# A time-warping kernel: lanes side by side instead of interleaved, one wait for the whole table, edge padding written first

## The reference

```
x = x + _L0_xattn_ref(ctx_1024, _layernorm(x))     # alignment by dynamic time warping
x = x + _L0_attn_ref(_layernorm(x), ...)           # a recurrence over time
x = x + _L0_ffn_ref(_layernorm(x), ...)            # 8 experts, 2 for each row, and a shared one
```

```
R[i, j] = D[i, j] + min(R[i-1, j], R[i, j-1], R[i-1, j-1])
```

## Time and profile before

| | us |
|---|---|
| median of three runs | 1157.94 |
| the three runs | 1157.61, 1157.94, 1163.07 |
| the profiled execution | 1163.07, of which its span 1161.8 |
| busy: PE, DVE, ACT, POOL | 1008.3, 660.2, 494.6, 116.0 |
| chain that ended last: PE, DVE, DMA | 58%, 27%, 5% |

### The profile page before, as it was taken

How to read it: one execution, slowest core, us unless ns; L and a number is a source line. 1 busy time by engine, 2 the same in 40 slices (tenths; PEclk the granted TensorE clock), 3 DMA queues, 4 the chain that set the end, 5 groups by cost and what they waited for, 6 DMA issues and landing times.

```text
span 1161.8 us, 15564 instructions
## 1 busy us (share of the span) xinstructions
PE 1008.3 (87%) x4892; PEld 599.0 (52%) x4892; DVE 660.2 (57%) x2312; ACT 494.6 (43%) x847; POOL 116.0 (10%) x150
## 2 busy tenths in 40 slices
PE   5887779888881999967989699887999999999998
PEld 2332233333330555533766465556676767676776
DVE  4987889999999774686679312447211111111116
ACT  4886647767760545323321364332222222222221
POOL 1000000000000000000000000000343434342110
PEclk9999889999995999989889798897999999999999
DMA  9999764655758998250140393783222212123014
GB/s 355 262 315 358 246 213 142 185 162 169 234 180 282 286 300 249 82 163 0 30 159 1 120 357 115 193 323 118 67 71 67 75 61 81 57 85 107 28 59 177
DMA packets 123887, 189.76 MB, mean 163 GB/s; under 512 B 9232, under 2 KB 93360, under 8 KB 123808
## 3 DMA queue, kind: packets, MB, share of 16 engines
q1 hardware_dynamic: 117920, 170.41, 45.4%
q0 software_dynamic: 5888, 18.36, 5.0%
HBM read 165.43 MB, written 23.30 MB: 162 GB/s over the span
## 4 chain that ended last, share of the span: by engine, by line
PE 58%; DVE 27%; DMA 5%; issue 4%; ACT 3%; SPq 2%; POOL 0%; DVEq 0%; ACTq 0%; POOLq 0%
PE bank L1824 13%; PE bank L1671 8%; PE bank L1855 7%; PE bank L1692 5%; DVE table L832 4%; PE bank L1816 3%; PE bank L1835 3%; DVE beyond L848 2%; PE bank L1847 2%; DVE passed L853 2%; PE bank L1598 2%; DVE col_min L825 2%; DMA spaced<-dist 2%; DVE z L762 2%; PE bank L1599 2%
## 5 line engine op out<-in xcount | busy, mean ns | idle before, releaser
L1036 DVE TENSOR_TENSOR hid<-bank,act_s 128x352 f32<-128x352 f32 x104 | 54.2, 523 | 221.1 <-PE bank L1824 182.2
L1824 PE MATMUL bank<-w_up,srcT 128*128 x512 | 162.8, 460 | 0.7 <-ACT srcT L1442 0.7
L1450 ACT ACTIVATE act_s<-bank 128x352 f32<-128x352 f32 x104 | 48.1, 464 | 200.7 <-PE bank L1824 127.6
L1582 PE MATMUL bank<-sq,ones 128*64 128x402 f32 (+1 forms) x512 | 103.6, 527 | 30.1 <-ACT sq L1299 30.1
L1824 PEld LDWEIGHTS bank<-w_up,srcT 128*128 128x128 f32 x512 | 96.0, 189 | 47.9 <-issue 4.1
L1576 PE MATMUL bank<-ctxT,latT 128*64 128x402 f32 (+1 forms) x512 | 103.1, 525 | 6.0 <-DMA ctxT<-ctx_tr_dram 5.2
L1598 PE MATMUL bank<-table,ident 128*128 128x402 f32 x144 | 66.0, 541 | 47.1 <-DVE stays L795 41.6
L1299 ACT ACTIVATE sq<-ctxT 128x1608 f32<-128x1608 f32 x64 | 97.5, 1527 | 9.9 <-DMA ctxT<-ctx_tr_dram 9.9
L1671 PE MATMUL bank<-rows_c,on_path 128*64 128x256 f32 (+1 forms) x832 | 99.0, 389 | 2.2 <-DMA rows_c<-ctx_nat_dram 1.4
L1855 PE MATMUL bank<-w_dn,hidT 128*128 (+1 forms) x384 | 93.6, 380 | 0.4 <-DVE y_sb L1050 0.4
L832 DVE TENSOR_TENSOR_SCAN table<-col_min,table 128x201 f32<-128x201 f32 x140 | 88.6, 633 | 2.7
(11 more groups left out here) (293 smaller groups left out, 1625.0 us busy)
## 6 DMA issues: line engine op xcount, KB each, us to landing
rows_c<-ctx_nat_dram SPq DMA_DIRECT2D x32, 896.0 KB
ctxT<-ctx_tr_dram SPq DMA_DIRECT2D x32, 804.0 KB, 7.1
ctxT<-ctx_tr_dram SPq DMA_DIRECT2D x32, 797.0 KB, 7.0
rows_c<-ctx_nat_dram SPq DMA_DIRECT2D x32, 640.0 KB
spaced<-dist SPq DMA_DIRECT2D x128, 101.0 KB, 3.4
table<-spaced SPq DMA_DIRECT2D x64, 202.0 KB, 4.0
w_up<-w_t_dram SPq DMA_DIRECT2D x16, 704.0 KB, 12.6
w_dn<-w_t_dram SPq DMA_DIRECT2D x16, 256.0 KB, 5.3
```

The source lines that it names most:

```text
L1036: e.tensor_tensor(hid[i][:, :], psum[2 * i + 1][:, 0:HH], act_s[i][:, :], ALU.mult).then_inc(hid_done, 1)
L1582: last = e.matmul(ps[b * T:(b + 1) * T, 0:nq], ones[:, 0:T], sq[i][:, b, k, 0:nq], start=False, stop=(k == KC - 1))
L1824: last = e.matmul(psum[2 * i + m][:, 0:HH], srcT[t % 2][:, k, :], w_up[:, bass.ds(ex, 1), m, k, columns], start=(k == 0), stop=(k == KC - 1))
```

## The change

Three things change together.

1. **Lanes.** A batch's 8 segments now stand in 8 neighbouring partitions: partition p holds segment p % 8 of batch p // 8. The shuffles' tables (`LEFT`, `RIGHT`, `FIRST_LANE`) and the few instructions that derive a lane's segment and batch from its number follow; one DVE instruction on 128 x 1 is gone (`SHAPED` 14 to 13). A table load now writes neighbouring partitions: after pair 3 the 64 partitions 0 to 63 by one DMA for each 8 rows instead of two, after the others 32.
2. **One semaphore for the table.** `table_in` counts all pieces of a group together, and `align` waits once, before its first step, until all of them have landed.
3. **Padding.** `far` has 128 partitions of 7 * 202 numbers instead of 16 of 8 * 202. Two DMAs write the first 7 rows and the last 7 rows of every lane of `spaced`, before any distance, and the first store of a distance waits for them. `load_table` no longer waits for the padding.

```diff
-QUADS = P // 32
-SETS = GB // QUADS
-
-LEFT = [(lane - SETS) % 32 for lane in range(32)]
-RIGHT = [(lane + SETS) % 32 for lane in range(32)]
-FIRST_LANE = [lane % SETS for lane in range(32)]
+LEFT = [lane - 1 if lane % SEGS else lane + SEGS - 1 for lane in range(32)]
+RIGHT = [lane + 1 if lane % SEGS < SEGS - 1 else lane - SEGS + 1 for lane in range(32)]
+FIRST_LANE = [lane // SEGS * SEGS for lane in range(32)]
...
-PAD = SEGS * W
+PAD = (SEGS - 1) * W
...
-        TABLE_IN = [16 * SETS * (g + 1) for g in range(GROUPS)]
-        PADDED = 16 * (SEGS - 1)
+        TABLE_IN = [16 * -(-STEPS // FEW_ROWS) * sum(len(sets) for sets in LOADED_WITH[:g + 1]) for g in range(GROUPS)]
+        PADDED = 16 * 2
...
-            e.memset(far[0:GB, :], BIG).then_inc(filled, 1)
+            e.memset(far[:, :], BIG).then_inc(filled, 1)
...
+                e.wait_ge(table_in, TABLE_IN[g])
                 for step in range(STEPS):
-                    if step % FEW_ROWS == 0:
-                        e.wait_ge(table_in[step // FEW_ROWS], TABLE_IN[g])
...
                 e.wait_ge(dist_done, u + 1)
+                if u == 0:
+                    e.wait_ge(padded, PADDED)
                 if u == GUNITS:
-                    for c in range(ROW_CHUNKS):
-                        e.wait_ge(table_in[c], TABLE_IN[0])
+                    e.wait_ge(table_in, TABLE_IN[0])
...
-                sets = range(2 * first // QUADS, (2 * pair % GB + 2) // QUADS)
+                p0, p1 = 2 * first * SEGS, (2 * pair % GB + 2) * SEGS
                 e.wait_ge(cleared, g + 1)
-                e.wait_ge(padded, PADDED)
                 for i in range(DISTS):
                     e.wait_ge(dist_out[i], dist_slot_value(QUARTERS * pair + i))
-                for c in range(ROW_CHUNKS):
-                    r0, r1 = c * FEW_ROWS, min(STEPS, (c + 1) * FEW_ROWS)
-                    for i in sets:
-                        e.dma_start(table[g][i:P:SETS, 1 + r0:1 + r1, :].rearrange("p r c -> p (r c)"),
-                                    spaced[32 * i:32 * (i + 1), r0 * W:r1 * W]).then_inc(table_in[c], 16)
+                for r0 in range(0, STEPS, FEW_ROWS):
+                    r1 = min(STEPS, r0 + FEW_ROWS)
+                    e.dma_start(table[g][p0:p1, 1 + r0:1 + r1, :].rearrange("p r c -> p (r c)"),
+                                spaced[p0:p1, r0 * W:r1 * W]).then_inc(table_in, 16)
                     yield
...
-            def store_pads():
-
-                e.wait_ge(filled, 1)
-                for s in range(SEGS - 1):
-                    e.dma_start(bass.AP(spaced.tensor, s * LANE + (T + s) * W, [[SEGS * LANE, GB], [1, PAD]]),
-                                far[0:GB, :]).then_inc(padded, 16)
-
+            e.wait_ge(filled, 1)
+            e.dma_start(spaced[:, 0:PAD], far[:, :]).then_inc(padded, 16)
+            e.dma_start(spaced[:, T * W:LANE], far[:, :]).then_inc(padded, 16)
...
-                if u == QUARTERS:
-                    store_pads()
```

More of the change, by code:

```diff
@@ L75 @@
 HALF_RSQRT_MAGIC = float(0x5F3759DF - 0x00800000)
-QUADS = P // 32
-SETS = GB // QUADS
-LEFT = [(lane - SETS) % 32 for lane in range(32)]
-RIGHT = [(lane + SETS) % 32 for lane in range(32)]
-FIRST_LANE = [lane % SETS for lane in range(32)]
+LEFT = [lane - 1 if lane % SEGS else lane + SEGS - 1 for lane in range(32)]
+RIGHT = [lane + 1 if lane % SEGS < SEGS - 1 else lane - SEGS + 1 for lane in range(32)]
+FIRST_LANE = [lane // SEGS * SEGS for lane in range(32)]
 LOADED_WITH = [{3: 0, 5: 4, 7: 6}, {1: 0, 3: 2, 5: 4, 7: 6}]
 FEW_ROWS = 8
-ROW_CHUNKS = -(-STEPS // FEW_ROWS)
 LANE = STEPS * W
-PAD = SEGS * W
+PAD = (SEGS - 1) * W
 LN_INCS = 2 * CTILES + 1 + 6 + CTILES
@@ L97 @@
 LATENTS_AT = {6: 1, 13: 2, 20: 3}
-SHAPED = 14
+SHAPED = 13
 BACK_INCS = 1 + 3 * STEPS + (STEPS - T)
@@ L503, in build @@
         dist_out = [sem(f"dist_out{i}") for i in range(DISTS)]
-        filled, padded, third_clear = sem("filled"), sem("padded"), sem("third_clear")
-        table_in = [sem(f"table_in{c}") for c in range(ROW_CHUNKS)]
+        filled, padded, table_in, third_clear = sem("filled"), sem("padded"), sem("table_in"), sem("third_clear")
         step_done, stayed, gapped, barred, edged, coded, back_done, termed, spread = (
@@ L675, in vector_program @@
             e.wait_ge(built, BUILT)
-            e.tensor_scalar(seg_i[:, :], lane_i[:, :], SETS.bit_length() - 1, SEGS - 1, ALU.logical_shift_right,
-                            ALU.bitwise_and).then_inc(set_up, 1)
+            e.tensor_single_scalar(seg_i[:, :], lane_i[:, :], SEGS - 1, ALU.bitwise_and).then_inc(set_up, 1)
             e.wait_ge(set_up, 1)
@@ L868, in row_features @@
                 n = Tally()
-                e.tensor_scalar(lane_b[:, :], lane_i[:, :], SETS - 1, QUADS.bit_length() - 1, ALU.bitwise_and,
-                                ALU.logical_shift_left).then_inc(shaped, 1)
-                e.tensor_single_scalar(seg_i[:, :], lane_i[:, :], 5, ALU.logical_shift_right).then_inc(shaped, 1)
+                e.tensor_single_scalar(lane_b[:, :], lane_i[:, :], SEGS.bit_length() - 1,
+                                       ALU.logical_shift_right).then_inc(shaped, 1)
                 e.tensor_scalar(pick[:, :], expert_io[:, 0:SEGS], seg[:, 0:1], None, ALU.is_equal).then_inc(shaped, 1)
-                e.wait_ge(shaped, n(3))
+                e.wait_ge(shaped, n(2))
                 yield
-                e.tensor_tensor(own_b[:, :], lane_b[:, :], seg_i[:, :], ALU.add).then_inc(shaped, 1)
+                e.tensor_copy(own_b[:, :], lane_b[:, :]).then_inc(shaped, 1)
                 e.tensor_tensor(pick_x[:, :], pick[:, 0:1], pick[:, 1:2], ALU.add).then_inc(shaped, 1)
```

## The result

The changed kernel takes 1173.1 us (median of four runs, 1171.23 to 1176.99) against 1158.11 for the kernel before. The ratio is 1.0137, with a 95% interval of 1.011 to 1.0163: slower by 15.9 us (12.7 to 18.9) by the ratio and by 15.0 between the medians. The forecast was +12.2 us, 1170. The profiled execution after took 1176.62 us, of which its span 1175.4, 13.6 more than the span before. Both profiled executions are slower than their medians, by 3.5 us after and by 5 before.

The account below looks back on a forecast made before the run. The prediction took DVE's row to set the pace up to 366 us. Its terms, 8.5 + 2.6 - 0.9 + 2.0 = +12.2 us, on the median of 1157.94 gave 1170 us (forecast case 1165 to 1177), range 1160 to 1181.

Parts of the forecast that it names:

- The one wait at half rate: DVE's first table step, at 146.94 us, waits for all nine pieces at an estimated 203 GB/s: +8.5 us.
- The first table load: Stores behind the 3.67 MB load come 9.1 us later by data, 6.4 earlier by issue: +2.6 us of DVE waiting.
- the credit of 6.4 us: At the first table load, nine issues instead of 18 free SP 6.4 us earlier, so stores behind gain that.
- The load after pair 5: Table load at 120 us: 3.4 us more data than issue time, taken as covered, 0; without cover +3.4.
- the ring: Four tiles in the first stage, said to let a store be some 11 us late before DVE waits.
- The padding: Slow padding DMAs leave SP's row at 34.08 us, saving DVE's third wait for a store: -0.9 us.
- Group 1's table loads: Between 280 and 366 us, two pieces ahead of each of two context loads on the chain: +2.0 us.
- The last table load: Issued from 351.65 us, complete at 364.9, before DVE starts the second table at 366.17: cost 0, 1.3 us spare.
- the first stage becomes the DMA's: Rival: longer transfers fill the DMA engines from 20 to 146 us, 127 of 126 us; 1180 us, chance 0.17.
- Not slower: Rival: partition place doesn't matter to large packets; one wait costs 6.2, store waits of 6.6 vanish: 1157.5 us, chance 0.13.
- a quarter of the rate: Rival: 32 neighbours get no more than 16 did, +17 and +4 at the two tables: about 1190 us, chance 0.04.
- partly absorbed: Rival: PE and ACT run ahead, using part of DVE's 9 us idle between 146 and 280: 1160 to 1165, chance 0.08.

Follow-up runs that it names:

- the two other traces with the old padding: The kernel before with only one wait for the whole table (1166.7 us), and the kernel before with only neighbouring lanes (1168.35 us).
- the last experiment: The changed kernel with the first table load spread, two DMAs of 64 neighbouring partitions after each unit's store: 1170.04 us, ratio 1.0087.

## Why the prediction was right, step by step

- **The one wait at half rate**, +8.5: measured +8.4 (14.15 for 5.75), at 202 GB/s (203 was put in). The split is a little different: at the full rate the wait for all costs 7.0, not 6.2, and the half rate only 1.4 on top. From the first issue to the first table step 9.7 us pass in the experiment with one wait (from 144.18) and 10.9 in the changed kernel (from 149.92), 9.1 of these being 1.836 MB at 202 GB/s. (A KB of the rows is 1024 bytes and an MB a million, by which nine pieces make 1.836 MB.)
- **The first table load**, +2.6: measured +6.7 (from -2.8 at unit 20 to +3.9 at unit 22). This is the term that was mis-sized. The step that failed is the credit of 6.4 us for SP coming free earlier. The load took 9.6 us longer (24.6 for 15.0), 6.7 of them landed on DVE, so only 2.9 us were left of the credit. The first of the two stores was never late by SP alone: before, it was issued at 96.45, 3 us before the load was complete. What it waits for is the end of the data ahead of it, so an earlier issue only means a longer landing (17.3 us instead of 3.6). Where the 2.9 us come from is not shown; of the two waits only the second shrank, and before, the queue was just 75% to 77% busy from 97.8 to 100.2 us, when SP had come free. The experiment with the lanes alone has nearly the same waits, 12.7 us.
- **The load after pair 5**, 0: measured +1.6, at unit 30, within the stated +3.4. A store issued at 132.28 took 11.76 us to land there, just beyond the some 11 us that the ring was said to cover. That it covers less because the queue is late already is a reading that no run tests.
- **The padding**, -0.9: measured -2.4 up to unit 20 against this one trace of the kernel before. The store wait at 60 us (0.84) has gone, as forecast. The other 1.6 us are a shorter wait of DVE for PE at 70 us (3.10 us before, 1.51 after), and that one is shorter in the two other traces with the old padding too; from them the padding's part is 0.4 or 1.9 us. That the first store would start at about 31 without being missed was right: it was issued at 30.33. Alone, the padding brings nothing that can be measured.
- **Group 1's table loads**, +2.0: measured 0. The one context load left on the chain takes longer (9.38 us for 8.28) but the other has gone from it, and both tables start 13.9 us late. It needn't be 0: the changed kernel with the wait piece by piece is 5.8 us behind the kernel before at the first step of table 0 and 8.5 at that of table 1.

```profile
309.59 9.38 DMA ctxT<-ctx_tr_dram
```

- **The last table load**, 0: right. Its last piece is issued at 369.4 and lands 7.6 us later, at 377.0; DVE starts without a wait:

```profile
380.08 0.37 DVE L818 TENSOR_TENSOR col_min<-table 128x201 f32<-128x201 f32 x1
```

The sum, 8.4 + 6.7 + 1.6 - 2.4 = 14.3, less the 0.4 us by which the profile after began earlier, is the 13.9 of the trace; the forecast was 12.2, and the medians differ by 15.0. Misses of opposite sign (first load +4.1 and the load after pair 5 +1.6; the padding -1.5 and group 1 -2.0) mostly cancelled: the total is better than its terms, and that much of it was luck. The three parts alone measure +6.8, +8.8 and -1.6 us (the last can't be told from 0), 14.0 in sum, where the whole change has 15.9.

Of the rivals, "the first stage becomes the DMA's" was half right: its share did reach 1.00, and the last experiment shows that most of the transfer time is paid there wherever it stands, but what it costs is 6.7 + 1.6, not 12.5. "Not slower" and "a quarter of the rate" are out by the 202 GB/s, and of "partly absorbed" nothing shows up to the second table. The signs came as named: the wait of 14.15 us, the rate, the last piece 10.9 us after the first issue, SP done in 5.92 us, longer waits for stores, and the last distance of group 0 only 5.5 us later.

Behind the second table the shift didn't stay constant: +18.2 us at the last step of table 1, +13.6 at the end. Part of the rise is PE's clock. The same 28 products of the first context sum lie in these two rows (among 30 matmuls), the kernel before's first (the columns of the earlier trace rows, with the granted clock as the third number from the end):

```profile
379.60:382.90 3.30, 3.26 (x30) 2.01 (x31) 3.17 (x10) 1.68 (x3) 0.00 (x0) 1.00 1.07 335
```
```profile
394.60:399.60 5.00, 4.97 (x30) 2.85 (x31) 2.49 (x6) 1.67 (x3) 0.00 (x0) 0.66 1.10 342
```

Here the granted clock was at its full level of 2.4 GHz, there for the greater part at 1.2, and the 28 products took 4.9 instead of 3.2 us. In both PE had stood idle before the table's first products, 26.1 and 27.6 us. What gives 4.6 us back later wasn't tried; it lies in PE's stages behind 546 us. Some 3 us of it may be the slow execution of the kernel before: the one with the padding first, whose program is the same there, is 1.4 us ahead of it at the last step of table 1 and 4.2 at the end.

## What to carry to other kernels

A DMA's rate depends on which partitions it touches, and not only on how many: 32 or 64 neighbours have half of what the loads of 32 spread over all 128 partitions had here (202 to 213 for 406 GB/s). Where a mapping of work to partitions is free, choose the one that spreads every transfer, and wait for a transfer by the pieces in which it is consumed. When the DMA engines are full, price a transfer by when its data end, not by when the queue that issues it is free, and put large blocks between small urgent ones instead of ahead of them. At the full rate this took away 5.9 us of waiting (6.85 to 0.97); at half rate, with the engines full, 2.9 (14.1 to 11.2).

## What the runs showed that was not expected

- A load of 32 rows to neighbouring partitions is issued in 0.45 us (4.05 for nine), to partitions at a stride of 4 in 0.63 (5.67) and at a stride of 2 in 0.62; 64 neighbours take 0.62. Stores from 16 neighbours take longest, 0.79 (7.12 for nine).
- Loads that go in turn to partitions 0-31 and 64-95 take 9.5 us for nine pieces instead of 10.9, and run at 258 GB/s in the middle. "SBUF — State Buffer" of the Trainium skill, section "Can I just issue two DMAs to hit both halves?", has 6% for that; here it is 23% in the rate in the middle and 16% in the time of the nine (9.5 for 10.9 counted from the first issue), so consecutive DMAs do overlap somewhat.
- Loads of 16 rows at a stride of 8 take 7.4 us for nine, of which 5.6 are SP's issues, with the engines 60% busy, where 16 neighbours need 10.1.
